# Layer 1 cross attention: second unit's scores placed beside the attended values, transposes of y and routing placed later

## What is computed

```python
q = (Q @ Wq.T + bq).reshape(n, lq, H, D)
scores = jnp.einsum('nqhd,nkhd->nqkh', q, k) / jnp.sqrt(jnp.float32(D))
attn = jax.nn.softmax(scores, axis=2)
out = jnp.einsum('nqkh,nkhd->nqhd', attn, v)
return (out.reshape(n, lq, H * D) @ Wo.T + bo).reshape(n, lq, E)
```

## Time and profile before

| what | value |
|---|---|
| median of 3 runs | 2455.33 us (2452.11 to 2456.83) |
| the profiled execution's own time | 2453.8 us |
| its span, first to last instruction | 2452.1 us |
| PE busy | 2262.6 us (92%) |
| DVE busy | 1347.3 us (55%) |
| ACT busy | 1100.5 us (45%) |
| POOL busy | 849.8 us (35%) |
| mean granted clock of PE, share of full speed | 0.971 |

### The profile page before, as it was taken

One profiled execution on the slowest core, in us unless ns is written; L12 is line 12 of the kernel. 1 busy time (PEld: TensorE's weight loads), 2 busy tenths in 40 slices (PEclk: granted clock), 3 DMA queues, 4 the chain that ended last, 5 costly groups with the idle time before them and its releaser, 6 DMA issues. The chain is left out here.

```text
span 2452.1 us, 44501 instructions
## 1 busy us (share of the span) xinstructions
PE 2262.6 (92%) x17122; PEld 1768.8 (72%) x17122; DVE 1347.3 (55%) x2517; ACT 1100.5 (45%) x1872; POOL 849.8 (35%) x873
## 2 busy tenths in 40 slices
PE   7999998799998899999999799999995999999993
PEld 5777776466666566757776688888884888888893
DVE  6888888488887680015545567888885111111113
ACT  3666666456565564543334255555552111111113
POOL 3555454244444582000101234455444122222221
PEclk8999999899999999999999899999997999999997
DMA  5435554100110679480211323333332856666665
GB/s 144 113 90 129 137 128 115 61 27 27 53 53 19 214 254 295 149 262 4 69 50 37 112 90 106 104 104 109 104 121 76 293 174 191 193 174 183 194 203 148
DMA packets 204609, 313.21 MB, mean 128 GB/s; under 512 B 63473, under 2 KB 183153, under 8 KB 191089
## 3 DMA queue, kind: packets, MB, share of 16 engines
q1 hardware_dynamic: 184336, 255.25, 33.6%
q0 software_dynamic: 13440, 17.90, 4.1%
q10 hardware_dynamic: 6624, 37.23, 3.9%
HBM read 188.88 MB, written 121.45 MB: 127 GB/s over the span
## 5 line engine op out<-in xcount | busy, mean ns | idle before, releaser
L2748 ACT ACTIVATE dec_area<-me_ps_h 128x512 f32<-128x512 f32 (+1 forms) x160 | 88.7, 554 | 423.8 <-PE me_ps_h L2726 423.8
L2789 DVE TENSOR_SCALAR me_yo<-me_ps_y,moe_xg 128x256 f32<-128x256 f32 x72 | 34.8, 484 | 429.2 <-PE me_ps_y L2736 391.3
L2664 POOL DMA_INDIRECT xo<-me_yo,me_row x72 | 112.7, 1565 | 410.7 <-DVE me_yo L2789 350.2
L2726 PE MATMUL me_ps_h<-me_xt,me_w 128*128 128x256 f32 (+1 forms) x1056 | 210.1, 357 | 0.0
L2736 PE MATMUL me_ps_y<-me_w,dec_area 128*128 128x256 f32 x944 | 209.2, 379 | 0.7 <-DVE me_yo L2789 0.7
L2199 POOL TENSOR_TENSOR l1x_e<-l1x_e,l1x_ri 128x1024 f32<-128x1024 f32 x64 | 121.7, 1901 | 240.8 <-DVE l1x_ri L2459 240.8
L2736 PEld LDWEIGHTS me_ps_y<-me_w,dec_area 128*128 128x128 f32 x944 | 179.0, 190 | 24.8 <-issue 1.1
L2726 PEld LDWEIGHTS me_ps_h<-me_xt,me_w 128*128 128x128 f32 x1056 | 181.9, 191 | 20.0
L882 POOL TENSOR_TENSOR l0x_e<-l0x_e,l0x_ri 128x1024 f32<-128x1024 f32 x64 | 120.0, 1896 | 186.9 <-DVE l0x_ri L1102 186.9
L2298 PE MATMUL l1x_ps_p<-l1x_xct,dec_area 128*128 128x256 f32 x512 | 126.4, 392 | 1.0 <-ACT l1x_xct L2384 1.0
L2336 PE MATMUL l1x_ps_o<-dec_area,l1x_ot 128*128 128x256 f32 x512 | 120.4, 389 | 1.4 <-ACT l1x_ot L2407 1.4
(11 more groups left out here) (414 smaller groups left out, 5335.5 us busy)
## 6 DMA issues: line engine op xcount, KB each, us to landing
me_w<-in_w SPq DMA_DIRECT2D x33, 2048.0 KB, 9.5
xs<-dec_zero SPq DMA_DIRECT2D x31, 1032.0 KB
k<-kv_kt ACTq DMA_DIRECT2D x16, 1024.0 KB, 5.5
v<-kv_va ACTq DMA_DIRECT2D x16, 1024.0 KB, 5.2
l1x_kt<-k SPq DMA_DIRECT2D x16, 1024.0 KB, 5.1
l1x_va<-v SPq DMA_DIRECT2D x16, 1024.0 KB, 5.8
moe_w_first<-in_w SPq DMA_DIRECT2D x7, 2048.0 KB, 9.8
moe_xg<-xs SPq DMA_DIRECT2D x32, 258.0 KB, 2.8
```

The source lines that it names most:

```text
L2664: pool.indirect_dma_start(token_rows, bass.IndirectOffsetOnAxis(row[:, j % 2, q:q + 1], 0), yo[:, j % 2, q, :], None, compute_op=ALU.add). ...
L2726: last = pe.matmul(ps_h[i % HB][:, f % 2, 0:P * size(j)], weights(j)[:, FFN * c + f * P:FFN * c + f * P + P], xt[:, j % 2, c, 0:P * size(j ...
L2748: act.activation(h[:, j % 2, 2 * i:2 * i + 2, 0:P * size(j)], ps_h[i % HB][:, :, 0:P * size(j)], ACT.Gelu).then_inc(gelued, 1)
```

## The change

On PE the scores of unit 1 move from early in the step to directly ahead of `apply(n, 0)`, behind part 0 (even steps) or part 2 (odd steps) of the projection. The transposes of y move from the end of an even step (lag 4) to just behind the first scores of the next odd step (lag 5). The logits (`route`) move in the odd step from ahead of `multiply` to behind it. On ACT `copy_xr` follows the transposes of y to the odd step. No operation is added or removed, and the lists of DVE, POOL and SP are as before.

```diff
-                walk([(0, lambda n: score(n, 0)), (2, multiply), (-G, transposes), (6, lambda n: count(n // G)), (0, lambda n: score(n, 1)), (1, lambda n: transpose_e(n, 2)), (1, lambda n: transpose_e(n, 3))] +
+                walk([(0, lambda n: score(n, 0)), (2, multiply), (-G, transposes), (6, lambda n: count(n // G)), (1, lambda n: transpose_e(n, 2)), (1, lambda n: transpose_e(n, 3))] +
                      part(project_q, 0) +
-                     [(1, lambda n: apply(n, 0)), (0, lambda n: transpose_e(n, 0)), (0, lambda n: transpose_e(n, 1))] +
-                     part(project_q, 1) + [(1, lambda n: apply(n, 1)), (4, lambda n: transpose_y(n // G))],
-                     [(0, lambda n: score(n, 0)), (5, lambda n: route(n // G)), (2, multiply), (1, lambda n: transpose_e(n, 2)), (1, lambda n: transpose_e(n, 3)), (0, lambda n: score(n, 1))] +
+                     [(0, lambda n: score(n, 1)), (1, lambda n: apply(n, 0)), (0, lambda n: transpose_e(n, 0)), (0, lambda n: transpose_e(n, 1))] +
+                     part(project_q, 1) + [(1, lambda n: apply(n, 1))],
+                     [(0, lambda n: score(n, 0)), (5, lambda n: transpose_y(n // G)), (2, multiply), (5, lambda n: route(n // G)), (1, lambda n: transpose_e(n, 2)), (1, lambda n: transpose_e(n, 3))] +
                      part(project_q, 2) +
-                     [(1, lambda n: apply(n, 0)), (0, lambda n: transpose_e(n, 0)), (0, lambda n: transpose_e(n, 1))] +
+                     [(0, lambda n: score(n, 1)), (1, lambda n: apply(n, 0)), (0, lambda n: transpose_e(n, 0)), (0, lambda n: transpose_e(n, 1))] +
                      part(project_q, 3) + [(1, lambda n: apply(n, 1))])
```

More of the change, by code:

```diff
@@ L2431, in _ @@
                      part(bias_q, 0) + [(0, lambda n: copy_et(n, 0))] + part(bias_q, 1) +
-                     [(0, lambda n: copy_et(n, 1)), (4, lambda n: copy_xr(n // G))],
-                     [(2, lambda n: copy_ot(n, 1)), (0, lambda n: exponentials(n, 0)), (1, lambda n: copy_et(n, 2)), (1, lambda n: copy_et(n, 3))] +
+                     [(0, lambda n: copy_et(n, 1))],
+                     [(2, lambda n: copy_ot(n, 1)), (5, lambda n: copy_xr(n // G)), (0, lambda n: exponentials(n, 0)), (1, lambda n: copy_et(n, 2)), (1, lambda n: copy_et(n, 3))] +
                      part(bias_q, 2) +
```

## The result

The changed kernel takes 2478.47 us (median of four runs, 2475.86 to 2482.63) against 2454.51 for the kernel before: a ratio of 1.0099, 95% interval 1.008 to 1.0118. It is 24 us slower, where 2480 was forecast.

A forecast was written before the change was run, and what follows sets the result against it. PE was taken to bound the stage. Three waits less 0.32 us of saved work add 1.72 a pair, 20.6 over 12 pairs, plus 4 in the first pairs: 24.6 us slower, 2480, range 2468 to 2490.

The forecast's parts named there:

- counts, part 1: Even step: projection part 1 overwrites the counts, which DVE's placing reads only after unit 1's shift; wait of 1.07 us.
- logits, part 3: Odd step: projection part 3 waits for DVE to read the logits, behind unit 1's shift; wait of 0.64 us.
- x, part 0: Even step: projection part 0 waits for ACT's copy of x's transposes, in a chain from the odd unit 1 scores; 0.33 us.
- PE's own work: Summed piece lengths of a pair of steps without waits: 28.92 us against 29.24, with layout changes falling from 15 to 12.
- Scores followed by values: Unit 1 scores directly ahead of attended values on PE: 1.22 us, bounded by 1.09 and 1.55.
- (a): Wait for the counts ahead of projection part 1 in the even step: 1.07 us.
- (b): Wait for the logits ahead of projection part 3 in the odd step: 0.64 us.
- The first pairs: Pairs of steps before the twelve that have all three waits: 4 us lost, between 0 and 5.2.
- bias of part 3: On ACT, needed by the next even scores: hidden by the logits' wait, otherwise late by about 0.3 us.
- A change without waits: Rival: no wait appears, PE stays full and gains 5.1 us, to 2450.2; chance 0.04.
- The wait for the counts alone: Rival: logits and x come in time, only the counts' wait remains; 9.0 us slower, to 2464; chance 0.05.
- The clock: Rival: waits lower PE's granted clock; 2487 at a steady 0.98, 2500 with one deep fall in each pair; chance 0.06.

The follow-up runs named there:

- mended kernel: Changed kernel; before unit 1's shift DVE places counts' base (even), reads logits and first pick (odd); ACT's even exponential later, bias of part 3 earlier: 2450.66 us.
- half moves: Two kernels, y and logits moved as in the change, unit 1 scores moved only in even steps (2474.78 us) or only in odd steps (2454.23 us).
- placing first: Changed kernel with the first three operations of DVE's placing, which release the counts, ahead of unit 1's shift in the even step: 2475.76 us.
- DVE's lists: Changed kernel with DVE's base placing (even step), and logits and both expert picks (odd step), ahead of the shift of unit 1: 2463.79 us.
- DVE's and ACT's lists: Changed kernel with base placing, logits and both picks ahead of DVE's shifts, and ACT's even unit 1 exponential behind the bias of part 0: 2468.24 us.
- mended with old ends: Changed kernel with DVE's and ACT's lists reordered, but old PE and ACT order in two first steps; from step 30 ACT's list unmended, both picks before shift: 2446.34 us.

## Why the prediction was right

**The waits** stand where they were forecast, at the size worked out from the chains. Against the mended kernel, in which PE waits for nothing in a pair, they can be priced in full:

| in a pair | forecast | measured |
|---|---|---|
| counts, part 1 | 4.25 - 3.18 = 1.07 | 4.27 - 3.05 = 1.22 |
| logits, part 3 | 3.82 - 3.18 = 0.64 | 3.82 - 3.05 = 0.77 |
| x, part 0 | 6.63 - 6.30 = 0.33 | 6.56 - 6.36 = 0.20 |
| weights behind each wait | none | 3 x 0.10 = 0.30 |
| PE's own work | 28.92 - 29.24 = -0.32 | 28.59 - 29.24 = -0.65 |
| sum | +1.72 | 31.10 - 29.24 = +1.86 |

The 3.05 is 1571.83 - 1568.78 and the 6.36 is 1566.96 - 1560.60 in the mended kernel; the measured terms add to +1.84. The three chains were right to 0.07. Two terms were mis-sized, and they work against each other. **Scores followed by values** were priced at 1.22 from the end of the stage; in the pairs they take 1.09 (1517.86 - 1516.77). That row had a short wait in it: the values overwrite what DVE's residual (L2466) reads, and it read until 1845.55; at the same place in the kernel with y and the logits moved a wait of 0.30 for L2466 is printed. So it was no price of a change of layout. PE arrives 0.13 sooner at (a) and (b), which makes these waits longer and PE's work shorter. **The part behind a wait** takes 1.92 (1522.96 - 1521.04) instead of 1.82 (1568.78 - 1566.96), because its first weights are not loaded while PE waits: their load starts at 1521.04 with the matmul, and in the mended kernel at 1571.72 for a matmul at 1571.83. The sum had nothing for this.

**x's wait** was there, at a chain of the right length. That chain starts at the odd scores, and from it I took the odd move to be what makes x late. It is the even move that lays the wait open, as the half moves show.

**The first pairs** gave 4.86 for 4: 2.40 in the first, 1.24 and 1.21 in the next two. What was named is there: the projection waits for its inputs and the odd multiply for the evacuation. In the changed kernel's first steps:

```profile
1398.14 3.40 PE L2298 MATMUL l1x_ps_p<-l1x_xct,dec_area 128*128 128x256 f32 x8 [3.57 <-ACT l1x_xct L2384]
1409.78 1.09 PE L2317 MATMUL l1x_ps_e<-dec_ident,l1x_e 128*128 128x128 f32 x8 [3.30 <-POOL l1x_e L2199]
1434.76 3.72 PE L2336 MATMUL l1x_ps_o<-dec_area,l1x_ot 128*128 128x256 f32 x16 [1.25 <-ACT l1x_ot L2407]
```

**The end** was put at 0 and gave -2.9, since I had read the last pair for its waits and not for what stands in front of its last multiply. That the whole came out at 24.3 for 24.6 is luck in part: +0.9 in the first steps and 22.37 - 20.64 = +1.7 in the pairs are met by these -2.9.

**PE's busy time** was to fall by about 5 us in the stage. It did not: 464.45 against 464.57. The record of one matmul of a transpose is 0.27 long, at 0.11 from start to start, so the first part of each wait still counts as busy.

**Transposes of y cost nothing** only because the wait for the counts comes first; in the kernel with placing first they wait 0.36. The same holds for the bias of part 3, for which 0.3 was named and 0.25 came with DVE's lists.

**The rivals.** A change without waits would have given 28.59 a pair; it takes four edits of DVE's and ACT's lists to get there. The wait for the counts alone would have been 2464; the other two are in the trace. The clock stayed at 1.00 in the twelve pairs of every kernel; it was lower in the first steps and at the ends. The Trainium skill (TensorEngine Tiling (Array Packing), Performance Considerations) says that the evacuation of PSUM may become the bottleneck. The rows agree so far as each of the three waits is for DVE or ACT to have read a PSUM buffer; but DVE idled for 2.18 us while the counts lay ready, so for the longest of them the place in DVE's list and not its speed sets the time.

## What to carry to other kernels

An engine with no idle time says nothing of how near the others are: before a producer is moved later, work out for each consumer behind it on the in-order lists when it finishes and when the buffer is asked for again. A wait that goes may have covered another one, so price the next one before crediting the whole. Where a change is several moves, time them apart: here one diff held a part that makes the kernel 0.31% faster and one that makes it 1.34% slower, and the page shows neither.

## What the runs showed of the hardware that was not expected

- Scores (64 rows high) followed by attended values (64 columns wide) took 1.09 us, no more than scores followed by work on the whole array, both from start to start.
- Eight matmuls of 8 columns for the logits took 0.81 behind the multiply (1559.07 to 1559.88 in the kernel with DVE's and ACT's lists) and 0.92 between scores and multiply.
- A group of eight matmuls that begins behind a wait took 0.10 longer to its successor's start, at the full clock (1.92 against 1.82).
- Small operations of DVE can be held while POOL's scaling runs. In the changed kernel L2491 (128x16, two tensors read) took 1.76 us in the second pick of an expert and 0.17 in the first one (1536.79):

```profile
1539.16 1.93 POOL L2199 TENSOR_TENSOR l1x_e<-l1x_e,l1x_ri 128x1024 f32<-128x1024 f32 x1 [6.86 <-DVE l1x_ri L2459]
1539.36 1.76 DVE L2491 TENSOR_TENSOR l1x_big<-l1x_eq,l1x_prio 128x16 f32<-128x16 f32 x1
```

  It ends 0.03 behind POOL's operation. In the five kernels with a pick ahead of the odd shift L2491 took 0.17 throughout and L2490 of the first pick 0.70 instead; in the one with DVE's lists it started at 1553.44 and ended at 1554.14, again 0.03 behind POOL's (1552.22 + 1.89). In each of the 14 kernels 14 operations of these two kinds are held; every one ends 0.03 behind POOL's, and none that starts while POOL's runs stays short. So what is held is whichever of them starts in that time, and not a line. No run took POOL's work away.
- At the ends the granted clock during a multiply of 16 matmuls was 1.00, 0.69, 0.60 and 0.57 in four kernels (3.72, 5.41, 6.08 and 5.39 us; y and the logits moved, mended, mended with old ends, before). It is the last multiply in the first and the last of these and the one before it in the two mended ones. Idle times of 1.33, 2.79, 4.59 and 1.33 us stood ahead of it or of the logits just before it, so the idle time just before does not order them.
